# First attention batch prepared beside the last scan; row statistics of x1 taken in the attention phase

## The chip, the cores and the metric

The kernel runs on one core of a Trainium2 chip. The metric is the device time of one execution in microseconds (us); the figure compared is the median of several runs. TensorE is PE (PEld its weight loads), VectorE is DVE, ScalarE is ACT, GpSimd is POOL and SyncE is SP.

## What is computed

A decoder layer on x of 16 x 224 x 512, in float32. Cut to what matters:

```python
x = x + mamba(layernorm(x))                       # selective scan: 1024 channels, 16 states
x = x + cross_attention(layernorm(x), ctx, mask)  # 16 heads, 750 keys a batch
x = x + ffn(layernorm(x))                         # 512 -> 2048 -> 512, binarised weights, gelu
# mamba: xz = rmsnorm(r) @ W_in; x = silu(conv4(x)); dt, B, C = x @ W_x (dt through W_dt, softplus)
#        h_t = exp(dt_t*A)*h_{t-1} + dt_t*x_t*B_t; y = h.C + D*x; out = r + (y*silu(z)) @ W_out
# attention: softmax(q.k/sqrt(32) + mask*-1e9) @ v @ Wo + bo, k and v projected from ctx
```

## The kernel before

Three functions follow one another, each ended by a barrier of all engines: `mamba_phase`, `attention_phase`, `ffn_phase`. In each, every engine has its own program, written out as a loop over slots; what stands in which slot is fixed by lists, and an engine takes its instructions strictly in that order. Engines wait for each other through semaphores.

**Scan phase.** A batch has 32 slots (`SLOTS`), 512 in all (`ALL`). In slot g ACT computes the decays of slot g+1 (`decays`, L389), POOL the inputs (`inputs`, L709), DVE the scan (L608) and, in three of four slots, the product with C (L615); in the fourth POOL does it (`times_c`, L716). Every fourth slot PE sums the states of a tile (`sum_states`, L283; "the fold" here). DVE adds them to y (L623), POOL gates a batch's y with z (`gate`, L732), PE projects it with `w_out` (`out_proj`, L333, two halves), DVE adds the residual (L630), and `x1_stats` (L638, L641) takes mean and variance of the rows of the result x1, which SP stores. The front end of batch b+2 runs in the same slots: PE's projections (L305), `silus_x` (L464), `x_dbl` (L314), `keep_xd`, `dt_raw` (L323), `softplus_parts` (L488 to L493). Between them stand the projections of the keys and values of the attention, 192 units (`project_kv`, L348 and L352 on PE; `keep_kv`, L433 and L436 on ACT, a slot later). Their slots come from four lists; `usual` holds for windows 1 to 13, counted from slot 4 of a batch. Its last entry, 31, is slot 3 of the next batch, the slot of `x_dbl`.

**Attention phase.** A batch has 16 slots: `scores` (L1023) on PE, mask and minimum on DVE (L1212), exponential on ACT (L1130), three groups of transposes (L1039, `transpose_p`) in two PSUM banks, which ACT (L1139) and DVE (L1226, `keep_pT`) empty. Ahead of a batch, in slot -6, DVE normalises x1 (`normalise`, L1189), in slot -5 PE transposes it and ACT copies it (`keep_hT`, L1109), in slot -3 q is projected. `rstd_of_rows` computes all reciprocal deviations at the start from the statistics `mv1`; ahead of the loop stands `value_bias` (L999), which folds the bias of v through Wo.

## Time and profile before

| | |
|---|---|
| median of 3 runs | 3647.01 us (3641.19 to 3647.26) |
| the profiled execution | 3635.2 us, its span 3633.9 us |
| scan phase, to the last add of the residual | 0 to 1967.4 us |
| first `scores` of the attention | 2006.88 us |
| last add of the attention's residual | 3160.0 us |
| busy share of the span | PE 89%, DVE 73%, ACT 66%, POOL 49% |

The busy shares are means over phases with different limits; what an edit is worth is read in the phase that it touches. In a row, "[2.66 <-PE a_work L348]" says that the engine stood idle for 2.66 us ahead of this instruction, and what ended that.

### The profile page before, as it was taken

To read this page: it belongs to the slowest core of one execution; us is meant where nothing else is said; L and a number is where in the kernel's file an instruction comes from. 1 tells how busy PE (TensorE), PEld (TensorE's weight loads), DVE (VectorE), ACT (ScalarE), POOL (GpSimd) and SP (SyncE) were. 2 spreads that over 40 slices of the span, in tenths; PEclk is the share of its full clock that TensorE was granted. 3 is DMA by queue.
4 is the path that set the end of the run, shared out by engine and by line. 5 is a ranking of instruction groups with operands and counts; after the bars stand their busy time and mean duration, and the time that the engine had idled before them with its cause. 6 is when DMAs were issued, how large, how long until landed. Compare 5 with 4: busy or idle time off the path is not lost. (4 is left out here: it accounts for less than half of the span.)

```text
span 3633.9 us, 59573 instructions
## 1 busy us (share of the span) xinstructions
PE 3224.7 (89%) x20864; PEld 2265.2 (62%) x20864; DVE 2658.0 (73%) x4681; ACT 2385.3 (66%) x5276; POOL 1774.4 (49%) x1052
## 2 busy tenths in 40 slices
PE   5788988889888898889996899999999999789998
PEld 4556655666556665666553566666666666478887
DVE  2899999999999999999883666766776776422221
ACT  5777888778877888777862667766666676432222
POOL 2778887778878888778872000000000000045454
PEclk8899999999999999999998999999999999889999
DMA  6666665666666666676563032111211221111010
GB/s 169 169 171 185 188 164 149 178 189 183 164 156 177 188 172 157 171 191 183 154 166 120 35 97 72 58 45 50 81 48 45 73 62 45 42 46 44 24 47 24
DMA packets 286440, 425.14 MB, mean 117 GB/s; under 512 B 28641, under 2 KB 226273, under 8 KB 281538
## 3 DMA queue, kind: packets, MB, share of 16 engines
q1 hardware_dynamic: 273920, 410.75, 41.2%
q10 hardware_dynamic: 12226, 10.59, 1.0%
q8 instruction: 170, 2.79, 0.3%
q14 instruction: 124, 1.02, 0.1%
HBM read 320.25 MB, written 101.02 MB: 116 GB/s over the span
## 5 line engine op out<-in xcount | busy, mean ns | idle before, releaser
L709 POOL TENSOR_TENSOR a_hs<-a_rep,a_bmat 128x896 f32<-128x896 f32 x512 | 1061.5, 2096 | 314.7 <-PE a_yps L283 314.2
L389 ACT ACTIVATE a_states<-a_rep,a_a_neg 128x224 f32<-128x224 f32 x2048 | 793.7, 438 | 141.3 <-DVE a_hs L615 139.4
L608 DVE TENSOR_TENSOR_SCAN a_states<-a_states,a_hs 128x900 f32<-128x900 f32 x384 | 778.8, 2028 | 84.1 <-ACT a_states L389 82.0
L1212 DVE CUSTOM_DVE_ANT_0 b_sc<-b_sps,b_mask 112x375 f32<-112x375 f32 x1024 | 500.4, 545 | 143.7 <-PE b_sps L1023 143.5
L1039 PEld LDWEIGHTS b_tps<-b_ident,b_sc 112*125 112x125 f32 x3072 | 399.3, 189 | 277.8 <-issue 142.8
L1305 POOL TENSOR_TENSOR b_xt<-b_xt,b_bo 112x512 f32<-112x512 f32 x32 | 40.8, 1297 | 1060.6 <-DVE b_ln L1189 1060.6
L1039 PE MATMUL b_tps<-b_ident,b_sc 112*125 112x112 f32 x3072 | 489.1, 288 | 70.2 <-ACT b_sc L1130 46.0
L1130 ACT ACTIVATE b_sc<-b_sc,b_nmax 112x750 f32<-112x750 f32 x512 | 467.7, 915 | 52.1 <-DVE b_nmax L1218 52.1
L615 DVE TENSOR_TENSOR a_hs<-a_states,a_cmat 128x896 f32<-128x896 f32 x384 | 419.2, 1092 | 13.2
L305 PE MATMUL a_work<-a_hT,w_in 128*128 128x224 f32 x2048 | 418.5, 359 | 7.0 <-issue 4.6
L305 PEld LDWEIGHTS a_work<-a_hT,w_in 128*128 128x128 f32 x2048 | 390.9, 193 | 44.3 <-issue 38.3
L283 PE MATMUL a_yps<-a_hs,a_fold 128*32 128x224 f32 x4096 | 259.8, 401 | 120.3 <-DVE a_hs L615 53.6
L352 PE MATMUL a_work<-wv,ctx 128*125 128x512 f32 x768 | 353.8, 604 | 2.2 <-ACT kv_out L433 1.9
L348 PE MATMUL a_work<-ctx,a_wk 128*128 128x250 f32 x1536 | 347.8, 379 | 7.1 <-ACT kv_out L436 7.1
L1139 ACT ACTIVATE b_pT<-b_tps 125x448 f32<-125x448 f32 x512 | 274.5, 536 | 121.3 <-PE b_tps L1039 119.2
L348 PEld LDWEIGHTS a_work<-ctx,a_wk 128*128 128x128 f32 x1536 | 290.0, 191 | 57.5 <-issue 15.6
L283 PEld LDWEIGHTS a_yps<-a_hs,a_fold 128*32 128x32 f32 x4096 | 138.7, 120 | 243.5 <-issue 125.0
L1509 ACT ACTIVATE c_g<-c_fps,c_b,c_alpha 128x512 f32<-128x512 f32 x112 | 87.4, 781 | 279.2 <-PE c_fps L1452 279.2
L608 DVE TENSOR_TENSOR_SCAN a_hs<-a_states,a_hs 128x900 f32<-128x900 f32 x128 | 258.8, 2022 | 14.5 <-ACT a_states L389 14.5
L1556 DVE CAST c_gT_hi<-c_g 128x512 fp32r<-128x512 f32 x112 | 61.5, 549 | 269.2 <-ACT c_g L1509 269.2
L1591 POOL TENSOR_TENSOR c_gT_lo<-c_g,c_gT_hi 128x512 fp32r<-128x512 f32 x112 | 146.4, 1310 | 214.9 <-DVE c_gT_hi L1556 214.9
L716 POOL TENSOR_TENSOR a_hs<-a_hs,a_cmat 128x896 f32<-128x896 f32 x128 | 247.4, 1933 | 0.0
(143 smaller groups left out, 4925.0 us busy)
## 6 DMA issues: line engine op xcount, KB each, us to landing
a_rep<-du_scratch SPq DMA_DIRECT2D x512, 224.0 KB, 5.3
w_in<-W_in_dram SPq DMA_DIRECT2D x128, 512.0 KB, 4.5
du_scratch<-a_du SPq DMA_DIRECT2D x16, 1792.0 KB, 11.4
ctx<-ctxT_dram SPq DMA_DIRECT2D x48, 500.0 KB, 5.8
v_scratch<-kv_out SPq DMA_DIRECT2D x96, 250.0 KB
k_scratch<-kv_out SPq DMA_DIRECT2D x96, 250.0 KB, 4.5
b_keys<-k_scratch SPq DMA_DIRECT2D x16, 1500.0 KB, 11.5
b_v<-v_scratch SPq DMA_DIRECT2D x16, 1500.0 KB
```

The source lines that it names most:

```text
L283: mm = pe.matmul(yps[j * DG:(j + 1) * DG, tile % 2 * L:(tile % 2 + 1) * L], fold[:], hs[(G4 * tile + j) % RING][:, q, 1:ROW], start=(q == ...
L305: mm = pe.matmul(work[:, bank, j * L:(j + 1) * L], w_in[unit % WINS][:, k, j * P:(j + 1) * P], hT[:, k, :], start=(k == 0), stop=(k == KD ...
L348: mm = pe.matmul(work[:, bank, j * WIDE:(j + 1) * WIDE], wk[:, k, (2 * half + j) * P:(2 * half + j + 1) * P], keys[:, k, :], start=(k == 0 ...
L352: mm = pe.matmul(work[0:KC, bank, :], keys[:, k, half * KC:(half + 1) * KC], wv[:, k, :], start=(k == 0), stop=(k == KD - 1))
L389: e = act.activation(rows(states[:, g % DA, :])[:, q, 1:ROW], rep[tile % REPS][:, j, 0, :], ACT.Exp, scale=a_neg[:, g % SLOTS, q:q + 1])
L608: dve.tensor_tensor_scan(state if g % G4 else whole, state, whole, 0.0, ALU.mult, ALU.add).then_inc(S["scan"], 1)
L615: dve.tensor_tensor(hh[:, :, 1:ROW], rows(states[:, g % DA, :])[:, :, 1:ROW], cmat[b % 2][:], ALU.mult).then_inc(S["hc"], 1)
L709: pool.tensor_tensor(hs[g % RING][:, :, 1:ROW], rep[tile % REPS][:, j, 1, :].unsqueeze(1).broadcast_to([P, Q, L]), bmat[b % 2][:], ALU.mul ...
L1039: mm = pe.transpose(tps[0:KC, tile % 2, c * TT:(c + 1) * TT], sc[m // 2 % 2][:, 2 * (m % 2) + head, chunk * KC:(chunk + 1) * KC], ident[0: ...
L1130: act.activation(sc[block % 2][:, j, :], sc[block % 2][:, j, :], ACT.Exp, scale=-1.0, bias=nmax[:, block % 2, j:j + 1], accum_out=esum[:, ...
L1139: act.activation(place(m, pair), transposed(tile), ACT.Copy).then_inc(S["pt_act"], 1)
L1212: dve.tensor_tensor_reduce(out=sc[block % 2][:, j, cols], in0=sps[0:TT, j, 0:HALF], in1=mask[:, block % 2, cols], scale=-1.0, scalar=3.0e3 ...
```

## The change

Four things are done.

1. `Early` lays two sets of tiles over one piece of memory: tiles of the scan phase that are last used before its end, and the attention's first operands (keys, values, x1 of batch 0, wq, wo, mask, bq). In slots 20 to 26 of the last batch ACT issues their loads. Between the two halves of the last `out_proj` PE transposes the normalised batch 0, after DVE, POOL and ACT have taken its statistics, reciprocal deviation and difference. The last gate is split: six tiles in slot 511, two behind the last add.
2. `x1_stats` leaves the scan phase. In the attention DVE takes the statistics of each later batch in slot -6, ACT and POOL make the reciprocal deviation (`guess_rsqrt`, `rsqrt_of_rows`), DVE normalises in slot -5, PE and ACT transpose and copy in slot -4.
3. The last entry of `usual` is 30 and no longer 31.
4. `value_bias` moves into attention slot 3, its DVE parts into slots 2 and 5; identity, wq, wo, bq, mask, x1, keys and values of batch 0 are not loaded at the attention's start, nor the identity at the ffn's.

```diff
+    def __init__(self, mem, L, D, DI, R, N, KEYS, KC=125):
+        TT, KD, M = L // 2, D // P, DI // P
+        scan = (("w_x", [P, M, R + 2 * N]), ("w_dt", [R + 1, DI]), ("h", [TT, 2, D]), ("scan_hT", [P, KD, L]),
+                ("conv", [P, M, L]), ("du", [P, M, 2, L]), ("zs1", [P, M, L]), ("zs2", [P, M, L]),
+                *((f"scan_xt{i}", [TT, 2, D]) for i in range(3)))
+        attention = (("keys0", [P, KD, KEYS]), ("wq", [P, KD, D]), ("mask", [TT, 2, KEYS]), ("xt0", [TT, 2, D]),
+                     ("ln", [TT, 2, D]), ("hT", [P, KD, L]), ("bq", [P, KD]), ("mv", [TT, 2, 2]), ("var_eps", [TT, 2]),
+                     ("guess", [TT, 2]), ("tmp", [TT, 2]), ("rstd", [TT, 2]), ("stats", [TT, 2, 6]),
+                     ("v0", [KC, KEYS // KC, D]), ("wo", [P, KD, D]))
...
-        usual = (1, 3, 5, 12, 14, 18, 20, 22, 24, 26, 31)
+        usual = (1, 3, 5, 12, 14, 18, 20, 22, 24, 26, 30)
...
+                    if b == B - 1 and m == LAST:
+                        pe.wait_ge(S["gated"], B + 1)
...
+            def transpose_next():
+                pe.wait_ge(S["next_ln"], 1)
...
+                mm.then_inc(S["next_hT_ps"], 1)
...
+                    if b == B - 1 and slot - b * SLOTS == O_SLOTS[0]:
+                        transpose_next()
...
+            def wait_for_room():
+                for name, value in (("xd_ps", B), ("dt_ps", PAIRS * B), ("hT_ps", 2 * B), ("z_ps", PAIRS * B), ("dt", B),
+                                    ("u", B), ("part", PAIRS * B), ("gated", B - 1), ("du_out", 16 * B),
+                                    ("kv_out0", 16 * UNITS // OUTS), ("kv_out1", 16 * UNITS // OUTS),
+                                    *((f"xout{i}", 16 * (B // XS)) for i in range(XS - 1))):
+                    act.wait_ge(S[name], value)
+            def load_next(i):
+                dst, src, sem = (
+                    (early["xt0"][:], x1_dram[0].rearrange("(i p) d -> p i d", p=TT), "next_in"),
+                    (early["mask"][:], t["mask"].rearrange("(i p) k -> p i k", p=TT), "next_in"),
+                    (early["bq"][:], t["bq"], "next_bq"),
+                    (early["wq"][:], t["Wq"].rearrange("(k p) n -> p k n", p=P), "next_in"),
+                    (early["keys0"][:], k_dram[0], "next_in"),
+                    (early["v0"][:], v_dram[0].rearrange("(c p) d -> p c d", p=KC), "next_v"),
+                    (early["wo"][:], t["Wo"].rearrange("(k p) n -> p k n", p=P), "next_wo"))[i]
+                act.dma_start(dst, src).then_inc(S[sem], 16)
+            def guess_next():
+                act.wait_ge(S["next_var"], 1)
+                act.activation(early["guess"][:], early["var_eps"][:], ACT.Ln).then_inc(S["next_log"], 1)
+                act.wait_ge(S["next_log"], 1)
+                act.activation(early["guess"][:], early["guess"][:], ACT.Exp, scale=-0.5).then_inc(S["next_guess"], 1)
...
+                if slot == (B - 1) * SLOTS + 20:
+                    wait_for_room()
+                if slot - (B - 1) * SLOTS - 20 in range(7):
+                    load_next(slot - (B - 1) * SLOTS - 20)
...
+            guess_next()
+            keep_next()
...
-            def x1_stats(b):
-                dve.wait_ge(S["sum"], 2 * (b + 1))
-                if b:
-                    dve.wait_ge(S["x1"], b)
+            def stats_of_next():
+                dve.wait_ge(S["next_in"], 16 * 4)
                 for i in range(2):
-                    steps.after(dve.bn_stats(stats1[:, i, :], xt[b % XS][:, i, :]))
+                    steps.after(dve.bn_stats(early["stats"][:, i, :], early["xt0"][:, i, :]))
                 steps.settle()
                 for i in range(2):
-                    e = dve.bn_aggr(mv1[:, 2 * b + i, :], stats1[:, i, :])
-                e.then_inc(S["x1"], 1)
+                    e = dve.bn_aggr(early["mv"][:, i, :], early["stats"][:, i, :])
+                e.then_inc(S["next_stats"], 1)
+                dve.tensor_scalar(early["mask"][:], early["mask"][:], NEG_INF_SCALE, None, ALU.mult)
+                dve.wait_ge(S["next_bq"], 16)
+                dve.tensor_scalar(early["bq"][:], early["bq"][:], SCALE, None, ALU.mult)
+            def normalise_next():
+                dve.wait_ge(S["next_rstd"], 1)
+                dve.wait_ge(S["next_stats"], 1)
+                for i in range(2):
+                    e = dve.tensor_scalar(early["ln"][:, i, :], early["xt0"][:, i, :], early["mv"][:, i, 0:1],
+                                          early["rstd"][:, i:i + 1], ALU.subtract, ALU.mult)
+                e.then_inc(S["next_ln"], 1)
...
-                    if at == O_SLOTS[1] + 5:
-                        x1_stats(b)
+                    if b == B - 1 and at == SLOTS + 2:
+                        stats_of_next()
+                        normalise_next()
...
+            def gate_last(tiles, pairs):
+                b = B - 1
+                pool.wait_ge(S["y"], PAIRS * b + pairs)
+                pool.wait_ge(S["zs"], 2 * B)
+                pool.tensor_tensor(yT[b % 2][:, tiles, :], yT[b % 2][:, tiles, :], zs[b % ZS][:, tiles, :],
+                                   ALU.mult).then_inc(S["gated"], 1)
+            def rsqrt_of_next():
+                pool.wait_ge(S["next_stats"], 1)
+                pool.tensor_scalar(early["var_eps"][:], early["mv"][:, :, 1], EPS, None, ALU.add).then_inc(S["next_var"], 1)
+                pool.wait_ge(S["next_guess"], 1)
+                pool.wait_ge(S["next_var"], 1)
+                newton_rsqrt(steps, early["rstd"][:], early["guess"][:], early["var_eps"][:],
+                             early["tmp"][:]).then_inc(S["next_rstd"], 1)
...
+                if slot == ALL - 1:
+                    gate_last(slice(0, LAST), PAIRS - 1)
+                if slot == ALL + 4:
+                    gate_last(slice(LAST, M), PAIRS)
+                    rsqrt_of_next()
...
-        slots = range(-13, B * SLOTS + SLOTS // 2 + 1)
...
+        slots = range(-6, B * SLOTS + SLOTS // 2 + 1)
...
-            pe.wait_ge(S["weights"], 16 * 3)
-            value_bias()
             for slot in slots:
                 before = 2 <= slot <= N_ALL + 1
+                if slot == 3:
+                    value_bias()
...
-                    if at == -5:
+                    if at == -4 and b:
...
+            def guess_rsqrt(b):
+                act.wait_ge(S["row_var"], b)
+                act.activation(guess[:], var_eps[:], ACT.Ln).then_inc(S["row_log"], 1)
+                act.wait_ge(S["row_log"], b)
+                act.activation(guess[:], guess[:], ACT.Exp, scale=-0.5).then_inc(S["row_guess"], 1)
...
-                    if at == -5:
+                    if at == -5 and b:
+                        guess_rsqrt(b)
+                    if at == -4 and b:
...
+            def stats_of_x1(b):
+                dve.wait_ge(S[f"xin{b % 2}"], 16 * loads(b))
+                for i in range(2):
+                    steps.after(dve.bn_stats(stats1[:, i, :], xt[b % 2][:, i, :]))
+                steps.settle()
+                if b >= 2:
+                    dve.wait_ge(S["ln"], b - 1)
+                    dve.wait_ge(S["row_var"], b - 1)
+                for i in range(2):
+                    e = dve.bn_aggr(mv1[:, i, :], stats1[:, i, :])
+                e.then_inc(S["stats1"], 1)
             def normalise(b):
-                dve.wait_ge(S[f"xin{b % 2}"], 16 * (b // 2 + 1))
-                if b:
+                dve.wait_ge(S["stats1"], b)
+                dve.wait_ge(S["rstd"], b)
+                if b >= 2:
                     dve.wait_ge(S["unit"], unit_of["hT", b - 1, 1])
-                else:
-                    dve.wait_ge(S["rstd"], 1)
                 for i in range(2):
-                    e = dve.tensor_scalar(ln[:, i, :], xt[b % 2][:, i, :], mv1[:, 2 * b + i, 0:1],
-                                          rstd[:, 2 * b + i:2 * b + i + 1], ALU.subtract, ALU.mult)
+                    e = dve.tensor_scalar(ln[:, i, :], xt[b % 2][:, i, :], mv1[:, i, 0:1], rstd[:, i:i + 1],
+                                          ALU.subtract, ALU.mult)
...
-            dve.wait_ge(S["weights"], 16 * 3)
-            widen_bv()
             for slot in slots:
                 before = 2 <= slot <= N_ALL + 1
-                if slot == -6:
+                if slot == 2:
+                    widen_bv()
+                if slot == 5:
...
-                    if at == -6:
+                    if at == -6 and b:
+                        stats_of_x1(b)
+                    if at == -5 and b:
...
+            def rsqrt_of_rows(b):
+                pool.wait_ge(S["stats1"], b)
+                if b >= 2:
+                    pool.wait_ge(S["row_guess"], b - 1)
+                pool.tensor_scalar(var_eps[:], mv1[:, :, 1], EPS, None, ALU.add).then_inc(S["row_var"], 1)
+                pool.wait_ge(S["row_guess"], b)
+                pool.wait_ge(S["row_var"], b)
+                if b >= 2:
+                    pool.wait_ge(S["ln"], b - 1)
+                newton_rsqrt(steps, rstd[:], guess[:], var_eps[:], tmp[:]).then_inc(S["rstd"], 1)
...
-                    if at == -6:
+                    if at == -6 and b:
                         load_k(b)
-                    if at == -8:
+                    if at == -8 and b:
                         load_x1(b)
-                    if at == -4:
+                    if at == -4 and b:
...
-        for dst, src in ((ident[:], t["ident"]), (bq[:], t["bq"]), (bv[:], t["bv"])):
-            act.dma_start(dst, src).then_inc(S["weights"], 16)
-        act.dma_start(wq[:], t["Wq"].rearrange("(k p) n -> p k n", p=P)).then_inc(S["wq_in"], 16)
-        act.dma_start(wo[:], t["Wo"].rearrange("(k p) n -> p k n", p=P)).then_inc(S["wo_in"], 16)
+        act.dma_start(bv[:], t["bv"]).then_inc(S["bv_in"], 16)
...
-        for dst, src in ((b1[:], t["b1"]), (ident[:], t["ident"]), (b2[:], t["b2"].partition_broadcast(P))):
+        for dst, src in ((b1[:], t["b1"]), (b2[:], t["b2"].partition_broadcast(P))):
```

PE in the scan phase, around `x_dbl` (the row that reads w_x) of one batch, before:

```order
L283 MATMUL a_yps<-a_hs,a_fold 32x224 x16
L305 MATMUL a_work<-a_hT,w_in_50 128x224 x8
L314 MATMUL a_work<-a_du,a_w_x 96x224 x8
L352 MATMUL a_work<-wv,ctx_56 125x512 x4
L283 MATMUL a_yps<-a_hs,a_fold 32x224 x16
L348 MATMUL a_work<-ctx_56,a_wk 128x250 x8
```

and with the change:

```order
L310 MATMUL a_yps<-a_hs,a_fold 32x224 x16
L332 MATMUL a_work<-early_scan_hT,w_in_50 128x224 x8
L391 MATMUL a_work<-wv,ctx_56 125x512 x4
L341 MATMUL a_work<-early_du,early_w_x 96x224 x8
L310 MATMUL a_yps<-a_hs,a_fold 32x224 x16
L387 MATMUL a_work<-ctx_56,a_wk 128x250 x8
```

The unit of keys or values (a_work from wv and ctx) that came behind `x_dbl` now stands ahead of it; nothing else moves.

PE at the end of the scan phase and the start of the attention, before:

```order
L283 MATMUL a_yps<-a_hs,a_fold 32x224 x16
L333 MATMUL a_work<-a_w_out,a_yT 112x512 x16
L999 MATMUL b_ups<-b_wo,b_bv_wide 112x512 x4
L989 MATMUL b_ups<-b_ident,b_ln 128x112 x8
L1010 MATMUL b_ups<-b_hT,b_wq 128x224 x4
L1023 MATMUL b_sps<-b_keys,b_q_0 112x375 x8
L1010 MATMUL b_ups<-b_hT,b_wq 128x224 x4
L1023 MATMUL b_sps<-b_keys,b_q_0 112x375 x4
L1039 MATMUL b_tps<-b_ident,b_sc 125x112 x12
```

and with the change:

```order
L310 MATMUL a_yps<-a_hs,a_fold 32x224 x16
L362 MATMUL a_work<-a_w_out,a_yT 112x512 x8
L372 MATMUL a_states<-ident,early_ln 128x112 x8
L362 MATMUL a_work<-a_w_out,a_yT 112x512 x8
L1117 MATMUL b_ups<-early_hT,early_wq 128x224 x4
L1131 MATMUL b_sps<-early_keys_70,b_q_0 112x375 x8
L1117 MATMUL b_ups<-early_hT,early_wq 128x224 x4
L1131 MATMUL b_sps<-early_keys_70,b_q_0 112x375 x4
L1147 MATMUL b_tps<-ident,b_sc 125x112 x12
L1107 MATMUL b_ups<-early_wo,b_bv_wide 112x512 x4
L1131 MATMUL b_sps<-early_keys_70,b_q_0 112x375 x4
```

The transposes of batch 0 went between the halves of `out_proj`, and `value_bias` (the row with b_bv_wide) from ahead of the first `scores` to behind the first transposes of p.

ACT in the attention, ahead of a batch, from the copies of p (b_pT) on, before:

```order
L1139 ACTIVATE b_pT<-b_tps 125x448 x2
L1109 ACTIVATE b_hT<-b_ups 128x448 x2
L1130 ACTIVATE b_sc,b_esum<-b_sc,b_nmax 112x750
L1139 ACTIVATE b_pT<-b_tps 125x448
L1130 ACTIVATE b_sc,b_esum<-b_sc,b_nmax 112x750
L1139 ACTIVATE b_pT<-b_tps 125x448
```

and with the change:

```order
L1251 ACTIVATE b_pT<-b_tps 125x448 x2
L1223 ACTIVATE early_guess<-early_var_eps 112x2
L1225 ACTIVATE early_guess<-early_guess 112x2
L1242 ACTIVATE b_sc,b_esum<-b_sc,b_nmax 112x750
L1251 ACTIVATE b_pT<-b_tps 125x448
L1242 ACTIVATE b_sc,b_esum<-b_sc,b_nmax 112x750
L1251 ACTIVATE b_pT<-b_tps 125x448
L1242 ACTIVATE b_sc,b_esum<-b_sc,b_nmax 112x750
L1217 ACTIVATE early_hT<-b_ups 128x448 x2
L1242 ACTIVATE b_sc,b_esum<-b_sc,b_nmax 112x750
L1251 ACTIVATE b_pT<-b_tps 125x448 x2
```

The two small instructions on early_guess took the place of the copies into hT, which now come three rows of exponentials later.

## Rows read from the trace of the kernel before

**Rows 1.** Windows view: us; PE, PEld, DVE, ACT, POOL busy; PEclk; DMA share; GB/s.
```profile
1000.00:1116.00 116.00, 103.03 (x594) 71.60 (x593) 109.12 (x103) 92.83 (x214) 94.97 (x54) 0.96 0.65 172
1915.00:1925.00 10.00, 10.00 (x62) 6.23 (x61) 5.53 (x5) 6.98 (x18) 4.61 (x3) 1.00 0.37 112
1972.00:2007.00 35.00, 9.03 (x28) 4.54 (x32) 3.67 (x10) 1.88 (x5) 3.12 (x2) 0.60 0.79 240
```

**Rows 2.** Groups by line, DVE, 600 to 1528: busy us, mean ns, idle before.
```profile
L608 DVE TENSOR_TENSOR_SCAN a_states<-a_states,a_hs 128x900 f32<-128x900 f32 x192 | 389.3, 2028 | 36.9 <-ACT a_states L389 36.7 <-issue 0.2
...
L638 DVE BATCH_NORM_STATS2 a_stats<-a_xt 112x6 f32<-112x512 f32 x16 | 10.2, 680 | 0.0
```

**Rows 3.** Timeline, one scan batch, 1033 to 1048: start, us, engine.
```profile
1036.59 4.92 PE L314 MATMUL a_work<-a_du,a_w_x 128*96 128x224 f32 x16 [4.17 <-ACT a_du L464]
...
1041.35 3.55 PE L348 MATMUL a_work<-ctx,a_wk 128*128 128x250 f32 x16
...
1044.82 1.74 PE L283 MATMUL a_yps<-a_hs,a_fold 128*32 128x224 f32 x32
1044.93 0.83 ACT L433 ACTIVATE kv_out<-a_work,a_bk 128x250 f32<-128x250 f32 x2 [2.66 <-PE a_work L348]
...
1047.24 2.04 DVE L608 TENSOR_TENSOR_SCAN a_states<-a_states,a_hs 128x900 f32<-128x900 f32 x1 [1.21 <-ACT a_states L389]
```

**Rows 4.** Timeline, the same batch, 1053 to 1075.
```profile
1057.68 3.14 PE L283 MATMUL a_yps<-a_hs,a_fold 128*32 128x224 f32 x32 [3.35 <-POOL a_hs L716]
...
1062.03 0.54 ACT L488 ACTIVATE a_conv<-a_work 128x448 f32<-128x448 f32 x1 [3.29 <-PE a_work L323]
...
1066.02 7.03 PE L333 MATMUL a_work<-a_w_out,a_yT 128*112 128x512 f32 x16
...
1066.97 2.04 DVE L608 TENSOR_TENSOR_SCAN a_states<-a_states,a_hs 128x900 f32<-128x900 f32 x1 [1.22 <-ACT a_states L389]
```

**Rows 5.** Timeline, end of the scan phase, 1944 to 1968.
```profile
1945.88 3.95 POOL L732 TENSOR_TENSOR a_yT<-a_yT,a_zs 128x1792 f32<-128x1792 f32 x1 [9.48 <-DVE a_yT L623]
...
1949.98 16.71 PE L333 MATMUL a_work<-a_w_out,a_yT 128*112 128x512 f32 x32 [4.87 <-POOL a_yT L732]
...
1966.72 0.69 DVE L630 TENSOR_TENSOR a_xt<-a_xt,a_work 112x512 f32<-112x512 f32 x1 [6.18 <-PE a_work L333]
```

**Rows 6.** Timeline, start of attention, 1971 to 2008.
```profile
1971.76 0.33 SPq L1320 DMA_DIRECT2D b_xt<-x_scratch  x1
...
1974.46 2.48 ACTq L1366 DMA_DIRECT2D b_bo<-bo_dram  x1
...
1977.24 0.23 ACT L884 ACTIVATE b_row_guess<-b_row_guess 112x32 f32<-112x32 f32 x1
...
1994.85 6.16 PE L999 MATMUL b_ups<-b_wo,b_bv_wide 128*112 128x512 f32 x8 [28.16 <-DMA b_wo<-Wo_dram]
...
2006.88 0.90 PE L1023 MATMUL b_sps<-b_keys,b_q 32*112 32x375 f32 x8 [0.63 <-ACT b_q L1120]
```

**Rows 7.** Timeline, three attention slots ahead of batch 14, 2966 to 2984.
```profile
2967.63 0.66 PE L1039 MATMUL b_tps<-b_ident,b_sc 112*125 112x112 f32 x4 [1.09 <-DVE b_pT L1226]
...
2974.85 1.00 DVE L1189 TENSOR_SCALAR b_ln<-b_xt,mv,b_rstd 112x512 f32<-112x512 f32 x2 [0.80 <-DMA b_xt<-x_scratch]
...
2978.55 0.98 ACT L1109 ACTIVATE b_hT<-b_ups 128x448 f32<-128x448 f32 x2 [0.48 <-PE b_ups L989]
...
2979.01 0.62 DVE L1226 COPY b_pT<-b_tps 125x448 f32<-125x448 f32 x1
...
2980.48 0.69 PE L1039 MATMUL b_tps<-b_ident,b_sc 112*125 112x112 f32 x4 [0.32 <-ACT b_sc L1130]
...
2981.81 1.19 PE L1039 MATMUL b_tps<-b_ident,b_sc 112*125 112x112 f32 x8 [0.64 <-ACT b_sc L1130]
```

**Rows 8.** Timeline of POOL, 1060 to 1080.
```profile
1069.62 0.22 POOL L81 TENSOR_TENSOR a_ntmp<-a_guess 112x4 f32<-112x4 f32 x1
...
1070.77 0.21 POOL L697 TENSOR_SCALAR a_gain<-a_rsqrt 112x2 f32<-112x2 f32 x1
```

145 lines of the change are left out of this document (76 added, 69 removed).

## Prediction

> **What bounds the kernel now.** I read the windows first, to see which engine fills a stretch, then the groups of DVE, to see who ends its idle time, and then the timeline where a wait stands. In a steady scan batch of 116 us DVE is busy for 109.1, PE for 103.0, POOL for 95.0 and ACT for 92.8 [rows 1]: DVE's chain of scans sets the pace. It stands idle for 36.9 us in eight batches, 4.6 a batch, and decays from ACT end nearly all of it [rows 2]. The timeline tells why ACT is late. PE waits 4.17 us for `silus_x`, then runs `x_dbl` (4.92), then the keys' unit (3.55), then the fold of slot 3, which starts at 1044.82; ACT stands 2.66 us in front of the copy of that unit, with the decays of a scan queued behind it, and that scan comes 1.21 late [rows 3]. Later in the batch the fold waits 3.35 for POOL's product with C, ACT waits 3.29 for PE's `dt_raw`, and a scan comes 1.22 late [rows 4]. So the scan phase is a circle in which a wait of PE is handed on twice.
>
> At the phase's end everything stands in one line: POOL gates 3.95 us with PE idle, PE projects for 16.71, DVE adds at 1966.72 [rows 5]. Then comes a stretch that DMA bounds: from the start of the attention at 1971.76 to its first `scores` at 2006.88, 35.1 us, PE waits 28.16 for wo [rows 6], and is busy for 9.03 of 35 [rows 1]. In the attention PE is nearly always busy; its waits are 0.3 to 1.1 us, ended by DVE's and ACT's copies of p and by the exponentials [rows 7].
>
> **The entry 30 for 31.** The unit now stands ahead of `x_dbl` and is free to run in the 4.17 us in which PE waits for silu; it needs 3.55 [rows 3]. `x_dbl` starts where it did, and the fold behind it is issued 3.55 earlier, at about 1041.3. ACT's 2.66 us go, since the unit is done before ACT comes to it. POOL's part (the inputs that need y's folding, the squares, `times_c`) shifts with the fold, which removes most of the 3.35 that the next but one fold waits for POOL, and with it the 3.29 of ACT [rows 4]. The bound from above is DVE's whole idle time, 4.6 us a batch; from below it is the one stall next to the moved unit, 1.2. I followed the slots of one batch: with both stalls gone the scan of 1066.97 can start at about 1063.2, and behind it PE (103 of 116), ACT and POOL have room to stay ahead. I take 3.8 a batch. Thirteen windows: **-49** (bounds -16 and -60). What is late next is DVE itself, which then waits about 0.8 a batch.
>
> **`x1_stats` leaves the scan phase.** Two row statistics of 0.68 [rows 2] and their aggregates (0.12 together, an estimate from their share) are 1.48 us a batch on the engine that bounds; some 0.3 is taken by a wait for ACT that follows. 1.2 in thirteen batches: **-16** (bounds 0 and -22). In the last two batches, full of units of keys and values, I count nothing.
>
> **The phase's end.** Six of the eight tiles are gated ahead of the last fold; the last quarter costs about 1.0 instead of 3.95. PE starts its projection behind the fold, near 1946, where it now starts at 1949.98 [rows 5]. Thirty-two matmuls need 16.71 there [rows 5], but sixteen need 7.03 in the steady batch [rows 4], which is 14.1 for both halves; eight transposes add 1.2, if they cost what the eight transposes of p do [rows 7]. DVE's last add then comes about 6.2 earlier, at 1960.5. From the end of that add, 1967.4, to the attention's first instruction at 1971.76 [rows 6] lie 4.3 us of the last store and the barrier, which stay. **-6** (bounds -3 and -8).
>
> The Trainium skill, in "TensorE: Matmul & The Clock Gate", Part 1, says that TensorE is throttled by default and that activity releases it, so an idle stretch ahead is paid for with slower matmuls. The rows above agree: after 4.87 us of idle time 16.71 instead of 14.1. By that rule the halves stay slow if the normalised rows come late and PE waits between them, and the sum would be 2.6 us higher.
>
> **The attention's start.** Nothing of batch 0 is loaded any more. ACT issues bv, bo (2.48) and copies the first q [rows 6], PE's eight q matmuls lie beside that: about 3.6 us from the phase's start to the first scores instead of 35.1, **-31.5**. `value_bias` is still PE work, now at full clock in slot 3: half of 7.03 [rows 4] for its eight matmuls, **+3.5**; in the idle stretch it cost 6.16 [rows 6] and hid behind loads. One issue fewer at the ffn's start: **-0.6**. With the end of the phase the boundary gives **-35**.
>
> The early loads are 6.3 MB: keys and values 1.54 each, wq and wo 1.05 each, mask 0.67, x1 0.46. Beside the last scan the transfers take a share of 0.37 at 112 GB/s [rows 1], so a full share is about 300 GB/s and the free 0.63 carries 190. From the first issue (slot 20 of the last batch, about 1905 us) to the end of the projection are 55 us, room for 10 MB. I take them as hidden. ACT's seven issues fall in slots where it has 3 us free in 10 [rows 1]. The Trainium skill, "DMA: Bandwidth & Descriptors", section "Issuing engines are not separate DMA queues", speaks against it: ACT's loads share the same 16 DMA engines with SP's transfers. The share in the rows already counts all queues, so I leave the sum, but the rule is the base of a rival.
>
> **The attention's batches.** Fifteen batches get the statistics (1.48) in slot -6, where DVE now normalises for 1.00 after a wait of 0.80 for x1 [rows 7]; that slot stays as it is. In slot -5 the normalisation waits for a chain across three engines. ACT is free at 2978.07 (the copy at 2978.55 less its wait of 0.48) [rows 7]; Ln and Exp at 0.23 each [rows 6] end at 2978.6; a handover costs 0.15 (POOL's 1945.88 and 3.95 against PE's 1949.98) [rows 5]; POOL's Newton steps take 1.15 [rows 8]; so DVE starts at 2980.05 instead of having finished, and ends at 2981.05. Behind it on DVE stands `keep_pT`, 0.62, now 2979.01 [rows 7]: it ends at 2981.7, and PE, which waits for that bank and goes on at 2980.48 today, goes on at 2981.85: +1.4. The transposes of h (0.93) move to the next slot, where they fill the wait of 0.64: +0.3. Together 1.7 a batch, **+25**. Bounds: 0.6, if DVE's lateness is mostly made up where PE waits anyway, to 3.0, if ACT's later copy of h delays exponentials too; +9 to +45. The nearest row for a PE that finds DVE busy with statistics ahead of the copy is 1.09 [rows 7].
>
> **Sum.** -65 in the scan phase, -35 at the boundary, +25 in the attention: -75. The profiled execution took 3635.2, so 3560; the median of the runs is 11.8 above it, so **3572**.
>
> **Rivals.** Forecast as above: 0.50; its own range is 3558 to 3588.
> A. The stall comes back at the next place where ACT is short, and the entry 30 gives 1.2 a batch instead of 3.8. For it: DVE waits for ACT at two places of the batch, and moving ACT's work earlier moves no capacity. Against: ACT has 23 us free in 116. 34 less: 3606. Chance 0.20.
> B. The attention loses 0.6 a batch. For it: PE waits already at these slots. 3556. Chance 0.12.
> D. It loses 3.0 a batch: 3592. Chance 0.08.
> E. The early loads hold up the keys' and values' stores and the loads of ctx in the last batch. If they take the DMA engines for themselves, 6.3 MB at 300 GB/s are 21 us; the free share makes it unlikely. 3593. Chance 0.05.
> C. The other side: the wait for the reciprocal deviation costs a whole slot each time and more. It decides from 100 us, 6.7 a batch; a slot is 4.5 (from 2006.88 to the last add at 3160 in 16 batches of 16 slots), and the loss of one whole slot in each batch would be 68 instead of 25, still 32 faster in all. For it: POOL's own work in that slot could lie ahead of the chain. At 7.5 a batch it gives 3572 - 25 + 113 = 3660. Chance 0.05, with it the case that the moved unit is not ready in time and nothing is won in the scan phase.
>
> **How the numbers follow.** B and A lie at 3556 and 3606, and with the bounds of the boundary (about 5) and errors of the scan terms the range 3545 to 3612 leaves out less than 2 in 10. Changes under 0.2%, about 7 us, can hardly be told from none. Forecast, A, B, D and E are all faster: 0.95; of C 0.03 is slower and 0.02 within 0.2%.
>
> **What the profile of the changed kernel would show.** Period of a scan batch 111 us instead of 116, DVE's idle time ahead of scans near 1 us a batch; `x_dbl` without a wait of 4.17 and shorter than 4.92; ACT without its waits of 2.66 and 3.29. First scores 3.5 to 4 us behind the attention's first instruction; no DVE or ACT wait for a DMA in the last scan batch. In the attention a wait of about 1 us of the normalisation for POOL, and one of PE for DVE's b_pT of 1 to 1.5, once a batch, with the period up by 1 to 2 from 72 (1153 us in 16 batches). It is wrong if PE still waits ahead of `x_dbl` for more than the unit fills, if DVE waits for ACT in other slots as long as before, or if a store of keys lands late.

## The result and the profile after

The changed kernel takes 3606.26 us (median of 4 runs, 3603.87 to 3619.08) against 3644.66 for the kernel before beside it (median of 4): ratio 0.9902, 95% interval 0.9877 to 0.9928. It is 1.0% faster, 38 us, where 75 were forecast. The time lies in the range, but the gain is half of the forecast.

The table cuts each profiled execution at the same events. "13 windows" runs from the first residual add of batch 0 to that of batch 13, "batch 14" to that of batch 14, "last" to the second add of batch 15, "boundary" to ACT's first copy of q, "attention" to the last minimum over scores, "rest" to the end. The numbers are differences of start times in the timelines; e1 to e14 are the experiments below.

| kernel | 13 windows | batch 14 | last | boundary | attention | rest | span |
|---|---|---|---|---|---|---|---|
| before | 1510.3 | 103.6 | 86.4 | 39.6 | 1131.5 | 496.1 | 3633.9 |
| changed | 1472.6 | 103.8 | 92.5 | 8.7 | 1163.6 | 495.5 | 3603.7 |
| e1 | 1477.9 | 104.1 | 85.3 | 39.4 | 1140.6 | 496.3 | 3614.8 |
| e2 | 1507.8 | 103.6 | 92.4 | 8.6 | 1162.8 | 496.2 | 3639.6 |
| e3 | 1478.6 | 104.1 | 91.2 | 8.6 | 1164.5 | 496.5 | 3614.5 |
| e4 | 1484.9 | 104.1 | 79.5 | 8.6 | 1164.2 | 495.7 | 3603.8 |
| e5 | 1478.4 | 104.1 | 90.9 | 8.6 | 1161.1 | 496.8 | 3611.6 |
| e6 | 1475.6 | 104.1 | 79.5 | 8.6 | 1166.4 | 496.4 | 3605.0 |
| e7 | 1462.4 | 103.5 | 92.3 | 8.6 | 1182.4 | 496.8 | 3611.9 |
| e8 | 1466.9 | 104.1 | 91.1 | 8.6 | 1159.6 | 492.6 | 3590.5 |
| e9 | 1475.2 | 104.1 | 79.5 | 8.7 | 1138.7 | 496.5 | 3572.7 |
| e10 | 1480.5 | 104.1 | 92.2 | 8.6 | 1164.2 | 495.3 | 3613.4 |
| e11 | 1549.0 | 104.2 | 79.5 | 8.6 | 1143.0 | 495.1 | 3646.9 |
| e12 | 1475.5 | 104.2 | 79.6 | 8.6 | 1146.2 | 495.8 | 3580.6 |
| e13 | 1481.4 | 104.1 | 79.6 | 8.6 | 1152.6 | 496.2 | 3589.3 |
| e14 | 1462.2 | 104.0 | 79.8 | 8.7 | 1137.4 | 495.0 | 3557.5 |

Four kernels have the same code through the thirteen windows (changed, e4, e5, e6), and they took 1472.6 to 1484.9, mean 1477.9: below 12 us, one profile of this stretch decides nothing. Five more have this code with statistics of x1 in it (e1, e3, e9, e12, e13); they took 1475.2 to 1481.4, mean 1477.7. The attention of the kernel before, unchanged in e1, took 1131.5 and 1140.6, and that of e9, unchanged in e11 and e14, 1137.4 to 1143.0.

The change did around `x_dbl` what was forecast. The timeline of the changed kernel, one scan batch (answers to [rows 3, 4]):

```profile
1020.58 3.24 PE L341 MATMUL a_work<-early_du,early_w_x 128*96 128x224 f32 x16 [0.81 <-ACT early_du L505]
...
1023.75 1.74 PE L310 MATMUL a_yps<-a_hs,a_fold 128*32 128x224 f32 x32
...
1025.67 2.09 POOL L798 TENSOR_TENSOR a_hs<-a_rep,a_bmat 128x896 f32<-128x896 f32 x1 [2.20 <-PE a_yps L310]
...
1028.56 3.99 POOL L821 TENSOR_TENSOR a_yT<-a_yT,early_zs 128x1792 f32<-128x1792 f32 x1
...
1032.51 2.08 POOL L798 TENSOR_TENSOR a_hs<-a_rep,a_bmat 128x896 f32<-128x896 f32 x1
...
1034.54 1.93 POOL L805 TENSOR_TENSOR a_hs<-a_hs,a_cmat 128x896 f32<-128x896 f32 x1
...
1036.62 2.12 PE L310 MATMUL a_yps<-a_hs,a_fold 128*32 128x224 f32 x32 [3.36 <-POOL a_hs L805]
```

`x_dbl` waits 0.81 us instead of 4.17 and takes 3.24 instead of 4.92. But the later fold still waits 3.36 us for POOL's product with C, as in [rows 4], where the forecast let this wait go. POOL in the kernel before, between the same two folds:

```profile
1049.63 3.99 POOL L732 TENSOR_TENSOR a_yT<-a_yT,a_zs 128x1792 f32<-128x1792 f32 x1
...
1055.60 1.93 POOL L716 TENSOR_TENSOR a_hs<-a_hs,a_cmat 128x896 f32<-128x896 f32 x1
```

The first fold now starts 3.17 us behind `x_dbl` (1020.58 to 1023.75) instead of 8.23 (1036.59 to 1044.82). POOL's product came forward with it: from the first fold to the second lie 12.87 us, where it was 12.86 (1044.82 to 1057.68). But what PE has to do between the two folds, a unit, `dt_raw` and another unit, came forward with it too, so PE is at the second fold as early as ever before POOL's product is done. What makes the product late is in POOL's queue: the gate (3.99) and the inputs (2.08) stand ahead of it. ACT's wait of 3.29 for `dt_raw` is gone.

DVE's waits, four batches of each kernel (sum, times, longest), before:

```profile
DVE a_states L608 <- ACT a_states L389: 18.2, 16, 1.7
DVE a_yT L623 <- PE a_yps L283: 5.0, 4, 1.5
```

and changed:

```profile
DVE a_states L687 <- ACT a_states L430: 10.9, 16, 1.1
DVE a_states L687 <- POOL a_hs L798: 4.2, 4, 1.1
DVE a_hs L687 <- ACT a_states L430: 1.6, 4, 0.5
DVE a_work L674 <- ACT a_work L534: 1.5, 1, 1.5
```

A batch had 5.8 us of such waits (23.2 / 4) and has 4.6 (18.2 / 4), where the forecast left 0.8. The stalls went from their places and others came up, one of them behind POOL's inputs.

The last scan batch got longer, 92.5 instead of 86.4. ACT's waits of the changed kernel in its last 70 us of scans:

```profile
ACT kv_out L477 <- DMA v_scratch<-kv_out: 13.4, 3, 5.4
ACT kv_out L474 <- DMA k_scratch<-kv_out: 9.3, 2, 6.3
```

ACT stands 22.7 us in front of its copies of keys and values, until a store from the same buffer has landed; the decays stand behind it. In the same stretch of the kernel before, ACT waited for no DMA. The end of the phase and the boundary (answers to [rows 5, 6]):

```profile
1921.15 1.13 POOL L827 TENSOR_TENSOR a_yT<-a_yT,a_zs 128x448 f32<-128x448 f32 x1 [17.43 <-DVE a_yT L702]
...
1928.04 0.93 PE L372 MATMUL a_states<-ident,early_ln 112*128 112x112 f32 x8
...
1935.87 0.69 DVE L709 TENSOR_TENSOR a_xt<-a_xt,a_work 112x512 f32<-112x512 f32 x1 [6.95 <-PE a_work L362]
...
1941.12 0.33 SPq L1456 DMA_DIRECT2D b_xt<-x_scratch  x1
...
1944.52 0.45 ACT L1232 ACTIVATE b_q<-b_ups,early_bq 128x224 f32<-128x224 f32 x1 [14.53 <-PE b_ups L1117]
```

and PE there:

```profile
1920.31 7.89 PE L362 MATMUL a_work<-a_w_out,a_yT 128*112 128x512 f32 x16
...
1928.80 7.03 PE L362 MATMUL a_work<-a_w_out,a_yT 128*112 128x512 f32 x16
...
1945.02 1.61 PE L1131 MATMUL b_sps<-early_keys,b_q 32*112 32x375 f32 x8 [0.54 <-ACT b_q L1232]
```

The last quarter of the gate takes 1.13 us, the transposes 0.93, the halves of the projection 7.89 and 7.03 instead of 16.71 in all, and the first scores come 3.9 us behind the attention's first instruction instead of 35.1. In the windows view TensorE's granted clock is 0.72 from 1918 to 1925, over the end of the last fold and the first 5 us of the first half, with 9.65 us of idle time of PE ahead of that fold, and 1.00 from 1925 to 1936; in the kernel before it was 0.61 in the first 7 us of the projection, behind PE's 4.87 us of idle time, and 1.00 after. The Trainium skill, "TensorE: Matmul & The Clock Gate", Part 1, by which TensorE is throttled unless it has been active, agrees with both.

In the attention, ahead of batch 14 (answers to [rows 7]):

```profile
2940.42 1.29 DVE L1297 BATCH_NORM_STATS2 early_stats<-early_xt 112x6 f32<-112x512 f32 x2 [0.77 <-DMA early_xt<-x_scratch]
...
2941.74 0.25 DVE L1303 BATCH_NORM_AGGREGATE early_mv<-early_stats 112x2 f32<-112x6 f32 x2
...
2944.01 0.20 ACT L1225 ACTIVATE early_guess<-early_guess 112x2 f32<-112x2 f32 x1
...
2945.12 0.20 POOL L115 TENSOR_TENSOR early_rstd<-early_tmp,early_guess 112x2 f32<-112x2 f32 x1
2945.42 1.00 DVE L1312 TENSOR_SCALAR early_ln<-early_xt,early_mv,early_rstd 112x512 f32<-112x512 f32 x2 [0.55 <-POOL early_rstd L115]
...
2946.33 0.62 DVE L1348 COPY b_pT<-b_tps 125x448 f32<-125x448 f32 x1
...
2947.10 1.09 PE L1147 MATMUL b_tps<-ident,b_sc 112*125 112x112 f32 x8 [1.39 <-DVE b_pT L1348]
```

DVE waits 0.55 us for POOL, normalises, and only then runs `keep_pT`; PE waits 1.39 us for it. These rows look as the forecast drew them, 1.4 for PE. What they cost is another question, to which e5 answers.

### The profile page after: what moved, and what is told of

The parts are those of the page before. It is cut to its first block and busy times, and to the rows that moved or that the text cites. A ratio compares the mean times of both kernels' runs of the same rounds, so it can differ in the third digit from the quotient of the medians.

```text
span 3603.7 us, 59690 instructions
## 1 busy us (share of the span) xinstructions
PE 3227.3 (90%) x20864; PEld 2268.9 (63%) x20864; DVE 2657.5 (74%) x4676; ACT 2388.7 (66%) x5306; POOL 1791.1 (50%) x1133
## 5 line engine op out<-in xcount | busy, mean ns | idle before, releaser
L1334 DVE CUSTOM_DVE_ANT_0 b_sc<-b_sps,early_mask 112x375 f32<-112x375 f32 x1024 | 500.2, 546 | 151.2 <-PE b_sps L1131 151.0
L1147 PEld LDWEIGHTS b_tps<-ident,b_sc 112*125 112x125 f32 x3072 | 403.8, 192 | 290.4 <-issue 170.7
L1147 PE MATMUL b_tps<-ident,b_sc 112*125 112x112 f32 x3072 | 491.5, 290 | 82.7 <-DVE b_pT L1348 40.5
L332 PE MATMUL a_work<-early_scan_hT,w_in 128*128 128x224 f32 x2048 | 424.1, 362 | 6.4 <-issue 3.9
L332 PEld LDWEIGHTS a_work<-early_scan_hT,w_in 128*128 128x128 f32 x2048 | 395.2, 195 | 48.7 <-issue 42.0
L310 PE MATMUL a_yps<-a_hs,a_fold 128*32 128x224 f32 x4096 | 248.7, 387 | 115.0 <-POOL a_hs L805 46.0
L391 PEld LDWEIGHTS a_work<-wv,ctx 128*125 128x125 f32 x768 | 144.9, 192 | 169.3 <-issue 157.9
```

Of the source, the lines that this page charges most:

```text
L310: mm = pe.matmul(yps[j * DG:(j + 1) * DG, tile % 2 * L:(tile % 2 + 1) * L], fold[:], hs[(G4 * tile + j) % RING][:, q, 1:ROW], start=(q == ...
L332: mm = pe.matmul(work[:, bank, j * L:(j + 1) * L], w_in[unit % WINS][:, k, j * P:(j + 1) * P], hT[:, k, :], start=(k == 0), stop=(k == KD ...
L391: mm = pe.matmul(work[0:KC, bank, :], keys[:, k, half * KC:(half + 1) * KC], wv[:, k, :], start=(k == 0), stop=(k == KD - 1))
L1147: mm = pe.transpose(tps[0:KC, tile % 2, c * TT:(c + 1) * TT], sc[m // 2 % 2][:, 2 * (m % 2) + head, chunk * KC:(chunk + 1) * KC], ident[0: ...
L1334: dve.tensor_tensor_reduce(out=sc[block % 2][:, j, cols], in0=sps[0:TT, j, 0:HALF], in1=mask[:, block % 2, cols], scale=-1.0, scalar=3.0e3 ...
```

## Experiments

Ratios are to the kernel before; expectations are quoted as they stood before each run.

**e1 and e2: the entry 30 alone, and the change without it.** e1 is the kernel before, e2 the changed kernel:

```diff
 # e1
-        usual = (1, 3, 5, 12, 14, 18, 20, 22, 24, 26, 31)
+        usual = (1, 3, 5, 12, 14, 18, 20, 22, 24, 26, 30)
 # e2
-        usual = (1, 3, 5, 12, 14, 18, 20, 22, 24, 26, 30)
+        usual = (1, 3, 5, 12, 14, 18, 20, 22, 24, 26, 31)
```

> The kernel before with one number changed, the last entry of usual 30 instead of 31. The forecast priced it at 3.8 us in each of thirteen windows: about 49 us faster, ratio 0.987. Theory P, formed from the two profiles (a scan batch went from 116.0 to 113.2 with both edits, and the row statistics are 1.4 of that): 1.4 a batch, about 18 us faster, ratio 0.995. Rival R: the entry is worth something only once the statistics are gone; then no change, ratio 1.000.

> The changed kernel with the entry back at 31. Theory P: the changed kernel loses the same 1.4 a batch, 18 us slower than it, about 3624, ratio to before 0.995. The forecast's 3.8 would give 3655, ratio 1.003. Rival R (the edits work only together): more than 30 us slower than the changed kernel.

e1: 3615.08, ratio 0.9921 (0.9908 to 0.9935), 29 us faster by the ratio and 27 by the medians; thirteen windows 1477.9 instead of 1510.3. e2: 3640.62, ratio 0.9998 (0.9986 to 1.0011). Both ways the entry is worth 2.2 to 2.6 us a batch (29 / 13 and 34 / 13), between the forecast's 3.8 and the 1.4 of theory P; rival R falls, since the entry works with the statistics in place. e2 says more: without the entry the rest of the change is worth nothing in all, since the boundary's gain of 31 us is paid back in the last batch (6) and in the attention (22 to 31, against e1 and before).

**e3: the statistics taken again in the scan phase**, in the changed kernel, results unused:

```diff
+                    if b < B - 1 and at == O_SLOTS[1] + 5:
+                        spare_stats(b)
```

> The changed kernel with the row statistics and aggregates of x1 taken again by DVE in the scan phase, in their old slot, into tiles that nobody reads. If DVE bounds the scan batches, 1.5 us come back in each of 14 batches, less what a wait takes up: 17 to 21 us slower than the changed kernel, ratio to before 0.995. Rival: they lie in DVE's idle time (5 us a batch), and the time stays within 5 us of the changed kernel.

3614.40, ratio 0.9920 (0.9905 to 0.9935), an interval that overlaps the changed kernel's. The median is 8 us above the changed kernel's, but e5, whose scan phase has no statistics, lies as high (3612.93). The windows say more: five profiles with statistics have a mean of 1477.7, four without one of 1477.9; and with the entry 31, it is 1507.8 without them (e2) against 1510.3. So 1.5 us a batch on the busiest engine are worth 0 to 0.2, less than one profile can show. They lie in waits that DVE has anyway: from 500 to 950 us it waits 21.1 us in the kernel before and 26.3 in e2, so without the statistics the waits are longer by most of what these took.

**e4: the early loads later**, so that keys, v and wo are issued when the last unit has been projected:

```diff
-                if slot - (B - 1) * SLOTS - 20 in range(7):
-                    load_next(slot - (B - 1) * SLOTS - 20)
+                if slot - (B - 1) * SLOTS in (20, 21, 22, 24, 29, 30, 31):
+                    load_next((20, 21, 22, 24, 29, 30, 31).index(slot - (B - 1) * SLOTS))
```

> The changed kernel with the early loads put elsewhere: x1, mask, bq and wq in slots 20, 21, 22 and 24 of the last batch, keys, v and wo only in slots 29, 30 and 31, when the last unit of keys and values has been projected. Theory P: the last batch loses its time because the stores of keys and values land late beside the early loads (ACT waits 22.7 us for them in five places); without the collision ACT's waits for the stores go back under 3 us in all, the phase ends about 11 us earlier, ratio 0.987. Rival Q: the time is lost to ACT's issuing itself (3.04 us for wo) and to the split of the gate; then at most 3 us are won.

3601.54, ratio 0.9895 (0.9877 to 0.9914). By the times alone nothing is settled, since the thirteen windows of this profile were 12 us longer, with the same code. The last batch took 79.5 instead of 92.5, and 79.5 to 79.8 in the six others with this edit (e6, e9 and e11 to e14). ACT's waits in the same stretch of e4:

```profile
ACT kv_out L474 <- DMA k_scratch<-kv_out: 6.2, 1, 6.2
...
ACT kv_out L477 <- DMA v_scratch<-kv_out: 4.0, 1, 4.0
```

10.2 us instead of 22.7 (wq and the mask still run there; theory P had expected under 3). So 13 us were lost to the early loads of keys, v and wo, and rival Q, at most 3 us, falls. Against the 86.4 of before, the end of the phase is then 6.9 us shorter.

**e5 and e6: the normalisation behind `keep_pT`**; e6 with the loads of e4 as well:

```diff
                     if at == -6 and b:
                         stats_of_x1(b)
-                    if at == -5 and b:
-                        normalise(b)
...
                 if before:
                     keep_pT(slot - 2)
+                for b in range(1, B):
+                    if slot - b * SLOTS == -5:
+                        normalise(b)
```

> The changed kernel with one thing moved in the attention: DVE normalises x1 of the next batch behind keep_pT in slot -5, no longer ahead of it. The forecast's mechanism (the normalisation waits 0.5 us for POOL and takes 1.0, keep_pT stands behind it, PE waits 1.39 us for that bank) says that 1.4 us a batch come back in fifteen batches: 15 to 21 us faster than the changed kernel, about 3587, ratio 0.985. Rival: the 1.9 us a batch that the attention lost lie in the transposes of h in the later slot and in ACT's later copy; then nothing is won, ratio 0.990.

> The changed kernel with both repairs: the early loads of keys, v and wo in slots 29 to 31 (as in e4) and the normalisation behind keep_pT (as in e5). If both repairs hold, the last scan batch is 13 us shorter and the attention 15 to 21 us: about 3575 to 3580, ratio 0.981 to 0.983. If only the loads matter, about 3597, ratio 0.988.

e5: 3612.93, ratio 0.9913 (0.9899 to 0.9928), attention 1161.1; e6: 3602.05, ratio 0.9888 (0.9874 to 0.9902), attention 1166.4, against 1163.6 and 1164.2 (e4). The 15 to 21 us expected of this order did not come. PE's waits in the attention of the changed kernel:

```profile
PE b_tps L1147 <- DVE b_pT L1348: 40.5, 38, 1.4
PE b_tps L1147 <- ACT b_sc L1242: 29.8, 67, 0.6
```

and of e5:

```profile
PE b_tps L1147 <- ACT b_sc L1242: 42.2, 95, 0.6
PE b_tps L1147 <- DVE b_pT L1348: 25.5, 26, 1.3
```

The waits for DVE fall by 15 us, as the forecast's mechanism says, and those for the exponentials rise by 12. PE waits for whoever is last, and here another was close behind.

**e7, e8 and e10: work taken away in the scan phase** of the changed kernel. e7 leaves out half of the inner sum of the units of windows 1 to 13 on PE, e8 the gate of six of eight tiles on POOL, e10 most of ACT's copies of these units:

```diff
 # e7
-                    for k in range(KD):
+                    for k in range(KM):            # KM = KD // 2 for the units of usual
 # e8
-                pool.tensor_tensor(yT[b % 2][:], yT[b % 2][:], zs[b % ZS][:], ALU.mult).then_inc(S["gated"], 1)
+                pool.tensor_tensor(yT[b % 2][:, 0:2, :], yT[b % 2][:, 0:2, :], zs[b % ZS][:, 0:2, :],
+                                   ALU.mult).then_inc(S["gated"], 1)
 # e10
+                if len(first) <= n < UNITS * B - len(last_but_one) - len(last):
+                    e = act.activation(out[0:KC, 0:64], work[0:KC, bank, 0:64], ACT.Copy)
```

> The changed kernel with half of the matmuls of each unit of keys and values left out in windows 1 to 13 (only two of four pieces of the inner sum are taken): some 19 us less work for PE in each of thirteen batches, with ACT, DVE, POOL and the transfers unchanged. If PE's lateness feeds DVE's remaining idle time of 5.6 us a batch (through ACT's copies and the folds), the period falls from 113.2 to 108 to 110 and the kernel is 40 to 65 us faster than the changed one. If ACT and POOL keep DVE waiting by themselves, less than 15 us are won.

> The changed kernel with POOL's gate cut to two of eight tiles in all batches but the last (the other tiles are not multiplied with z): 2.9 us less work for POOL a batch. If POOL (95 us of 113) is part of the chain that keeps DVE waiting (1.0 us a batch ahead of one scan, 3.36 ahead of a fold), 15 to 40 us are won against the changed kernel. If not, it stays within 8 us of it, ratio 0.989 to 0.991.

> The changed kernel with ACT's copies of keys and values in windows 1 to 13 cut to 64 columns (the rest of the unit isn't copied): about 6 us less work for ACT in each of thirteen batches. Leaving out 19 us of PE's work a batch (e7) gave 0.9 us a batch, 2.9 us of POOL's (e8) 0.8. If it is ACT's decays that come late (2.7 of DVE's 4.5 us of waits a batch in the profile), the period falls by 2 to 3 us from 113.4: the thirteen windows take 1440 to 1455 instead of 1478, ratio 0.981 to 0.985. If DVE's own chain of dependent instructions sets the pace, it is under 1 us a batch, 1465 or more, ratio 0.987 or more.

Times 3611.68, 3601.97 and 3610.36, ratios 0.9909 (0.9892 to 0.9926), 0.9899 (0.9884 to 0.9914) and 0.9899 (0.9876 to 0.9922): none of the three is clear of the changed kernel's 0.9902. Thirteen windows took 1462.4, 1466.9 and 1480.5 against a mean of 1477.9 and a lowest of 1472.6. By the busy times of the windows view PE had 15 us less to do a batch (87 against 102; not the 19 expected, with the granted clock at 0.92 instead of 0.96), POOL 2.7 and ACT 5.3. By the windows PE's 15 were worth 1.2 us a batch, POOL's 2.7 were worth 0.8, ACT's 5.3 nothing. The amount of work of none of these three sets this period. In e8 one sees how a wait is passed on, here PE in 450 us of the changed kernel:

```profile
PE a_yps L310 <- POOL a_hs L805: 13.4, 4, 3.4
...
PE a_yps L310 <- DVE a_hs L694: 4.0, 3, 1.3
```

and of e8:

```profile
PE a_yps L310 <- DVE a_hs L694: 18.0, 9, 2.8
```

The folds' 13.4 us for POOL, one of 3.35 a batch, are gone, and 14 us more for DVE have come.

**e9: part 2 undone.** The loads as in e4; statistics in the scan phase as before, all reciprocal deviations at the attention's start, the normalisation in slot -6, transposes in -5:

```diff
+                    if at == O_SLOTS[1] + 5:
+                        x1_stats(b)
                     if b == B - 1 and at == SLOTS + 2:
...
-                    if at == -6 and b:
-                        stats_of_x1(b)
-                    if at == -5 and b:
+                    if at == -6 and b:
                         normalise(b)
...
+        rstd_of_rows(act, dve_steps, mem, S, mv1, rstd)
```

> The changed kernel with the early loads as in e4, and with part 2 of the change undone: DVE takes the statistics of x1 in the scan phase as before, all reciprocal deviations are computed once at the attention's start beside the q projections, DVE normalises in slot -6 and PE transposes in slot -5 as before. Theory N, by the phases of nine profiles: the statistics cost the scan phase 0 to 6 us (its thirteen windows took 1477.9 and 1478.6 with them, 1472.6 to 1484.9 without) and the chain in the attention costs it 20 to 24 us (1161 to 1166 against 1131 and 1141, 4.4 of it value_bias). So 17 to 24 us faster than e4: about 3580, ratio 0.982 to 0.984. The forecast's sum, by which part 2 costs 25 in the attention and gives 16 in the scan phase, would give 9 us: 3592, ratio 0.987.

3574.78, ratio 0.9813 (0.9799 to 0.9828): the fastest full kernel here, 31 us below the changed one. The attention took 1138.7 instead of 1164, the thirteen windows 1475.2. Theory N's price (17 to 24) was even a little low: 27 us against e4.

**e12 and e13: what in part 2 costs 25 us in the attention**, both on e9. e12 normalises in slot -5 and transposes and copies in slot -4, without statistics or chain; e13 takes the statistics in slot -6, results unused:

```diff
 # e12
-                    if at == -5 and b:
+                    if at == -4 and b:
                         transpose_h(b, 0)
...
-                    if at == -5 and b:
+                    if at == -4 and b:
                         keep_hT(b, 0)
...
-                    if at == -6 and b:
+                    if at == -5 and b:
                         normalise(b)
 # e13
                     if at == -6 and b:
+                        spare_stats(b)
                         normalise(b)
```

> e9 with the normalisation in slot -5 and the transposes and copies of h in slot -4, as in the changed kernel, but without the statistics in slot -6 and without the chain through ACT and POOL. The attention took 1138.7 in e9 and 1164 in e4 and the changed kernel. The forecast's mechanism says that the wait for POOL (0.5 us a batch) and the normalisation of 1.0 us ahead of keep_pT are what costs: then this kernel loses 10 to 17 us against e9, 3585 to 3592. Rival S: the 1.5 us of statistics and aggregates that DVE has to do in slot -6 are what costs; then it stays within 5 us of e9. Rival V: the later transposes and copies cost all 25 us, about 3600.

> e9 with the statistics and aggregates of x1 taken once more by DVE in attention slot -6, ahead of the normalisation, into tiles that nobody reads; no chain, no later slots. The attention took 1138.7 in e9, 1146.2 in e12 (later slots alone), 1164.2 in e4 (later slots, statistics and chain). If the statistics are the rest (rival S), it takes 1150 to 1158, and the kernel about 3590, ratio 0.985. If the waits for ACT and POOL are the rest, it stays within 4 us of e9: 3575 to 3579, ratio 0.981 to 0.982.

e12: 3583.22, ratio 0.9841 (0.9828 to 0.9854), attention 1146.2, 7.5 us more than e9. e13: 3590.81, ratio 0.9863 (0.9845 to 0.9882), attention 1152.6, 13.9 more. The windows view of the attention, in the order e9, e12, e13, e4, tells the two apart; its second and third number are the stretch and PE's busy time, the third last is the granted clock:

```profile
1937.48:3076.18 1138.70, 1058.06 (x9244) 724.85 (x9244) 783.42 (x2802) 773.47 (x1684) 40.09 (x32) 0.99 0.19 57
1938.53:3084.76 1146.23, 1063.85 (x9244) 727.32 (x9244) 781.43 (x2802) 773.04 (x1684) 40.23 (x32) 0.98 0.19 57
1940.56:3093.15 1152.59, 1056.69 (x9244) 726.03 (x9244) 802.62 (x2862) 773.71 (x1684) 40.15 (x32) 0.99 0.19 57
1943.92:3108.14 1164.22, 1068.92 (x9244) 734.33 (x9244) 802.08 (x2863) 779.81 (x1714) 54.97 (x107) 0.98 0.19 56
```

PE stands idle for 80.6 us in e9, 82.4 in e12, 95.9 in e13 and 95.3 in e4. So the statistics alone bring all of the idle time that part 2 adds (15 us), and the later slots and the chain over ACT and POOL next to none. The other 11 of the 25.5 us are PE's busy time: the same 9244 matmuls take 1058.1 us in e9 and 1068.9 in e4, at a granted clock of 0.99 and 0.98, and e12's 7.5 us are mostly of this kind. The kernel before and e1 differ in the same way with one code in the attention (1052.2 and 1060.9 busy, 79.4 and 79.7 idle), so no run shows that an edit caused it. e12 by itself, 8 us above e9 by the medians, lies between rival S (within 5) and the forecast's mechanism (10 to 17), while e13's attention of 1152.6 is inside the 1150 to 1158 of S. By the idle times rival S is right: what costs by waiting is the 1.5 us that DVE has to do ahead of its own copy of p in slot -6. In e9 PE waits 18.0 us for DVE's b_pT and 44.0 for the exponentials in the attention. The same of e13:

```profile
PE b_tps L1163 <- ACT b_sc L1258: 43.3, 95, 0.6
PE b_tps L1163 <- DVE b_pT L1371: 34.1, 30, 2.4
```

16 us more for DVE, and the waits for the exponentials stay: what is added ahead of the copy of p comes out as time.

**e11: ACT's copies two slots behind their units**, on e9:

```diff
-            kept_at.setdefault(slot + 1 + crowded, []).append(n)
+            kept_at.setdefault(slot + 2, []).append(n)
```

> e9 with one more edit: ACT copies every unit of keys and values two slots behind its slot instead of one. In e9 and in the changed kernel ACT stands up to 2.8 us in front of such a copy and of the taps, with the decays of a scan queued behind, and taking work off PE, POOL or ACT (e7, e8, e10) has given at most 1 us a batch. If it is the order of ACT's queue that makes the decays late, the DVE waits of about 3.5 to 4.5 us a batch shrink by 1.5 or more, 20 to 40 us in thirteen batches: 3535 to 3555, ratio 0.970 to 0.976. If PE then waits for a bank of work (three banks, held a slot longer) or the waits come from DVE's own chain through POOL, nothing is won or some is lost: 3570 to 3600, ratio 0.980 to 0.988.

3607.23, ratio 0.9932 (0.9905 to 0.9960), 32 us slower than e9. Its twelve times fall in two groups, eight from 3601 to 3611 and four from 3642 to 3649; the profile is of the upper one, so its 1549 for the windows is above what the median had. PE's waits in 450 us of e11:

```profile
PE a_work L392 <- ACT kv_out L475: 11.5, 4, 4.3
PE a_work L388 <- ACT kv_out L478: 10.4, 4, 4.0
PE a_yps L311 <- POOL a_hs L819: 10.1, 3, 3.4
```

22 us behind banks that ACT has not emptied, 5.4 in e9 (3.0 and 2.4). The expected second branch: the wait moved from ACT to PE, and worse.

**e14: POOL's product with C cut** to one of four rows, on e9:

```diff
-                pool.tensor_tensor(hh[:, :, 1:ROW], hh[:, :, 1:ROW], cmat[b % 2][:], ALU.mult).then_inc(S["hc_pool"], 1)
+                pool.tensor_tensor(hh[:, 0:1, 1:ROW], hh[:, 0:1, 1:ROW], cmat[b % 2][:, 0:1, :],
+                                   ALU.mult).then_inc(S["hc_pool"], 1)
```

> e9 with POOL's product with C (one scan in four) cut to one of four rows, the other rows not multiplied: 1.4 us less between scan and fold, 11 us less work for POOL a batch. Theory L: the scan batch is a circle (scan, POOL's product, fold, inputs, scan) and PE's wait of 3.34 us for that product is part of it: PE's wait shrinks to 2, DVE's waits by 1 to 2 us a batch, the thirteen windows take 1450 to 1465 instead of 1475.2, ratio 0.974 to 0.979. If the time between scan and fold does not matter, 1470 or more and ratio 0.981.

3564.15, ratio 0.9787 (0.9770 to 0.9804), windows 1462.2, 13 us less than e9, inside the 1450 to 1465 of theory L and outside its rival's 1470. DVE's waits in 450 us of e14:

```profile
DVE a_states L688 <- ACT a_states L431: 7.3, 8, 1.1
DVE a_work L675 <- ACT a_work L535: 3.0, 2, 1.5
```

10.3 against 14.1 in the same stretch of e9. Theory L holds for 1.0 of the 3.5 us a batch. PE's waits did not shrink as it said: those for POOL's product (13.4 us in 450) are gone, and those of the folds for DVE's a_hs went from 4.0 to 22.3, as in e8.

## Why the prediction was wrong

**The entry 30 (forecast -49).** The right place, and the rows around `x_dbl` came as drawn, but the size failed: 29 us (e1) to 34 (changed against e2). The step that failed is "POOL's part shifts with the fold, which removes most of the 3.35". POOL's part did shift with the fold, but PE's own work up to the next but one fold shifted as well, and a wait between two queues that both move stays: 3.36, set by the gate ahead of the product in POOL's queue. The step behind it failed too, that DVE is then left with 0.8 us of waits; it kept 4.6, and even where that wait of PE is gone (e8, e14) the period falls by 0.8 to 1.0 only, and PE waits for DVE instead; what sets the rest of the period is open. And the 4.6 that the forecast called DVE's whole idle time left out the 1.2 a batch for the fold at L623; it was 5.8. Rival A had this case, with too low a price for the entry (1.2 a batch). That its 3606 is the measured time is chance: its other terms are the forecast's.

**`x1_stats` (forecast -16).** Measured 0 to 2.5 in all. The step that failed is the rule behind it, that work on the busiest engine counts nearly in full (1.2 of 1.48). DVE is busy for 107.6 of 113 us, but it also waits, and 1.5 us of work in a batch with 4.6 to 5.8 of waits vanish in them.

**The phase's end (forecast -6).** -6.9 is measured once the loads are moved (79.5 against 86.4), and +6.1 in the changed kernel. The forecast's own terms give 1961.3 for the last add (1946, 14.1 and 1.2), not 1960.5.

**The early loads (forecast: hidden).** This step failed, and rival E was right in kind: 13 us (92.5 against 79.5), where rival E had 21 at most and 0.05 of the chances. A mean share of 0.37 [rows 1] said nothing about a store on whose landing ACT waits with a buffer reused two units later. The forecast named the transfers as a rival's base, but took no row of the stores of the last batch, 250 KB each, with ACT's copy behind them. The Trainium skill, "DMA: Bandwidth & Descriptors", section "Issuing engines are not separate DMA queues", says that loads of one engine meet the transfers of another on the same DMA engines, and this trace agrees, with ACT's waits for SP's stores at 22.7 us.

**The attention's start (forecast -31.5) and `value_bias` (+3.5).** Measured -30.9 (39.6 to 8.7), and 3.60 us for the eight matmuls in slot 3.

**The attention's batches (forecast +25).** Right as a sum, 25.5 us (e9 against e4), and wrong as a mechanism. The order of normalisation and `keep_pT` is worth nothing (e5, e6); the statistics in slot -6, which the forecast priced at nothing ("that slot stays as it is"), cost 13.9 (e13) and bring all of the added idle time of PE. The rest, 11 us of longer busy time at a lower granted clock, was in no term of the forecast, and its cause stays open.

**The sum.** The forecast's -75, with the entry at -34 instead of -49, the statistics at 0 instead of -16 and 13 for the loads, becomes -31; the profile shows -30.2. Two rivals, A and E, held at once; the forecast had priced each by itself, so that their sum lay outside its own branch.

What stays open: 2.6 us of DVE's waits a batch are left in e14, nearly all for ACT, and no run takes them away.

## What to carry to other kernels

In a pipeline of in-order queues the wait that an edit removes is worth only the distance to the next one, so walk the queue of every engine that feeds the place, not just the two that showed idle time; and work placed in a wait of the busiest engine is free (the statistics in the scan phase), while the same work on a less busy engine, ahead of a copy for which the busiest one waits, costs 0.9 of its 1.5 us each time (e13). A load moved into a busy phase is to be priced by the transfers there on whose landing somebody waits, not by the mean share of the DMA engines. Before a chain is spread over three engines to save 1.5 us of statistics on one, try the kernel that leaves them where they were: e9 is 1.9% faster than the kernel before, twice the change's gain.

## What the runs showed of the hardware

The same scan code settled on different batch periods in different executions: 113.2 with a 114.4 every fourth in the changed kernel, 113.2 and 115.5 in turn in e4. e11 showed two groups of times 1.1% apart within one kernel. And in e7, with PE's work in the scan phase cut, the mean granted clock of the whole execution was 0.936 against 0.957, and the attention, whose code was not touched, took 1182.4 instead of 1163.6, with a granted clock of 0.96 against 0.97; 14 of these 19 us are PE's longer busy time (1083.5 against 1069.6). No run shows why the clock was lower there.
